# The order of two matrix products per attention head on TensorE, in a four-layer kernel on one core

## The chip, the cores and the metric

The kernel runs on one core of a Trainium2 chip. The metric is the device time of one launch in microseconds. Before the change it is 380.82 us, the median of three runs (380.45 to 381.33). All times below are in us unless they are marked ns.

## The reference

Four residual layers work on x, of 4 batches, 256 rows and 256 columns, each after a layer normalisation: a quantised expert layer, a feed-forward layer with ternary weights, an attention over a small context, and a feed-forward layer with a shared and a routed part. The change is in the attention:

```
q = (text_hidden @ Wq).reshape(B, T_text, N_HEADS, HEAD_DIM).transpose(0, 2, 1, 3)
k = (vision_tokens @ Wk)...      # 8 key/value heads, each used by two of the 16 heads
v = (vision_tokens @ Wv)...
...
attn = softmax(scores / scale)
out = jnp.einsum('bhts,bhsd->bhtd', attn, v)
return out @ Wo                  # summed over the 16 heads
```

A batch has 256 text rows and 256 context rows of 128 columns. The kernel folds Wq with Wk and Wv with Wo before the first attention (a_hi and c_hi below), so a head needs neither keys nor values of its own.

## The kernel before

The four batches run one after the other, and in each the four layers. Every engine has its instructions written out by hand in one fixed order, and semaphores tie the engines together. Products are taken in fp32r on values that are split into a high and a low part, so one product is three passes: high by high, high by low, low by high. The high part is a ScalarE copy out of PSUM, and the low part is a VectorE subtraction that follows it.

The attention of a batch is a loop over its 16 heads. For head h TensorE does the following, in this order (lines 688 to 712):

- turn_probs(h): four 128x128 transposes of the normalised probabilities into the bank pt (L646).
- scores(h+2): six matmuls into a bank s (L626, and L634 for the low part of the queries).
- queries(h+4): six matmuls into half of the bank qa (L418), up to head 11.
- beside(h, 0): pieces of other layers, at a few heads. At head 5 it turns rounded rows of the next batch's expert layer, and at head 12 it forms that layer's second product, both in batches 0 to 2. At head 14 it is the last folded weight in batch 0 (prep_unit, L933) and in batches 1 to 3 a late chunk of the feed-forward layer of the batch before (ffn_up, twelve matmuls of L418 on yt_hi and yt_lo). At head 15 in batches 1 and 2 it is ffn_down of a late chunk.
- project(h-2), from head 2 on: six matmuls into the bank o, four on ut_hi (L681) and then two on ut_lo (L685).
- mix(m), after every odd head up to 13 and after heads 14 and 15: it multiplies the turned probabilities of the heads 2m and 2m+1 with the context into the bank u (L662, L666).
- beside(h, 1): further pieces.

What project reads is made after the mix. ScalarE copies the bank u to ut_hi (mix_hi, L1010; semaphore u_h), and VectorE then subtracts to get ut_lo (mix_lo, L1754; u_l). The pair of heads 2m and 2m+1 is mixed at the end of head 2m+1, and head 2m+2 is the first to project it. So project stands close behind its inputs at the even heads 2 to 14. At an odd head it reads what the even head before it has read already.

What queries writes is copied by ScalarE once a pair is complete, at odd heads (queries_hi, qa_hi), and then VectorE subtracts (queries_lo, qa_lo). At an odd head ScalarE's order is: the turned probabilities (pt_hi), queries_hi, other layers' work, the two exponentials of head h+2 (L1062), and at the next head mix_hi. VectorE's order is: the inverses of the row sums (L1743), mix_lo at an even head, probs_lo (pt_lo), the row minima of the scores (L1735), queries_lo at an odd head, then other layers' work. GpSimd normalises the probabilities (L1355).

Of the kernel before, what the change touches and what calls it, by code (L numbers as in the profile page):

```python
# [78 lines left out]
def build(nc, x_in, gu_in, guT_in, ctx_in, ctxT_in, mask_in, w12T_in, w3T_in, wqT_in, wkT_in,  # L79
          wvT_in, wo_in, routerT_in, gateT_in, upT_in, downT_in, out):  # L80
    with ExitStack() as ctx:
# [19 lines left out]
        def mix_unit(h):  # L101
            return h // 2 if h < H - 2 else h - PAIRS + 1

        def mix_heads(m):
            return (2 * m, 2 * m + 1) if m < PAIRS - 1 else (m + PAIRS - 1,)
# [306 lines left out]
        def _(pe):  # L412
# [173 lines left out]
            def queries(b, h):  # L586

                p = h // 2
                if h % 2 == 0 and p >= 1:
                    pe.wait_ge(S["qa_l"], PAIRS * b + p)  # L590
                if b == 0 and h >= 2 and h % 2 == 0:
                    pe.wait_ge(S["prep_lo"], prep_count(h))
                if b == 0 and h == 1:
                    pe.wait_ge(S["prep_lo"], PREP_BANKS.index("qa", 5) + 1)
                dst = bank["qa"][:, (h % 2) * T:(h % 2 + 1) * T]
                for k in range(ND):
                    last = split_mm(dst, a_hi[:, h, k, :], a_lo[:, h, k, :], xt_hi[:, k, :], xt_lo[:, k, :],
                                    k == 0, k == ND - 1)
                if h % 2 == 1:
                    last.then_inc(S["qa_mm"], 1)  # L600
# [11 lines left out]
            def scores(b, h):  # L612
                if b == 0 and h == 0:
                    pe.wait_ge(S["qa0_h"], 1)
                else:
                    pe.wait_ge(S["qa_h"], PAIRS * b + h // 2 + 1)
                if h >= 2:
                    pe.wait_ge(S["s_min"], NT * (H * b + h - 1))
                elif b == 0:
                    pe.wait_ge(S["prep_lo"], PREP_BANKS.index(("s0", "s1")[h], 4) + 1)  # L620
                dst = bank["s0"] if h % 2 == 0 else bank["s1"]
                ring, col = (h // 2) % 2, (h % 2) * T
                for t in range(NT):
                    cols = slice(col + t * P, col + (t + 1) * P)
                    for half in (cxT_hi, cxT_lo):
                        pe.matmul(dst[:, t * T:(t + 1) * T], qa_hi[:, ring, cols], half[:, :],  # L626
                                  start=(t == 0 and half is cxT_hi), stop=False, skip_group_check=True)
                if b == 0 and h == 0:
                    pe.wait_ge(S["qa0_l"], 1)
                else:  # L630
                    pe.wait_ge(S["qa_l"], PAIRS * b + h // 2 + 1)
                for t in range(NT):
                    cols = slice(col + t * P, col + (t + 1) * P)
                    last = pe.matmul(dst[:, t * T:(t + 1) * T], qa_lo[:, ring, cols], cxT_hi[:, :],  # L634
                                     start=False, stop=True, skip_group_check=True)
                last.then_inc(S["s_mm"], 1)

            def turn_probs(b, h):
                if b == 0 and h == 0:
                    pe.wait_ge(S["prep_lo"], PREP_BANKS.index("pt") + 1)  # L640
                if h >= 1:
                    pe.wait_ge(S["t_l"], H * b + h)
                for t in range(NT):
                    pe.wait_ge(S["s_norm"], NT * (H * b + h) + t + 1)
                    for s in range(2):
                        last = pe.transpose(bank["pt"][:, s * T + t * P:s * T + (t + 1) * P],  # L646
                                            prob[:, h % 2, t, s * P:(s + 1) * P], ident[:, :])
                last.then_inc(S["t_mm"], 1)

            def mix(b, m):  # L650

                heads, cols = mix_heads(m), mix_cols(m)
                pe.wait_ge(S["t_h"], H * b + heads[-1] + 1)
                if m >= 1:
                    pe.wait_ge(S["u_l"], MIXES * b + m)
                elif b > 0:
                    pe.wait_ge(S["shared_x"], b)
                else:
                    pe.wait_ge(S["prep_lo"], PREP_BANKS.index("u", 6) + 1)
                for s in range(2):  # L660
                    for half in (cx_hi, cx_lo):
                        pe.matmul(bank["u"][:, cols], half[:, s, :], pt_hi[:, s, cols], start=(s == 0 and half is cx_hi),  # L662
                                  stop=False, skip_group_check=True)
                pe.wait_ge(S["t_l"], H * b + heads[-1] + 1)
                for s in range(2):
                    last = pe.matmul(bank["u"][:, cols], cx_hi[:, s, :], pt_lo[:, s, cols], start=False, stop=(s == 1),  # L666
                                     skip_group_check=True)
                last.then_inc(S["u_mm"], 1)

            def project(b, h):  # L670
                if b == 0 and h == 0:
                    pe.wait_ge(S["prep_lo"], 2 * PAIRS - 1)
                elif b == 0 and h == H - 2:
                    pe.wait_ge(S["prep_lo"], 2 * PAIRS)
                elif h == 0:
                    pe.wait_ge(S["routed_x"], b)
                pe.wait_ge(S["u_h"], MIXES * b + mix_unit(h) + 1)
                at = (h % 2) * T
                for t in range(NT):
                    for half in (c_hi, c_lo):  # L680
                        pe.matmul(bank["o"][:, t * D:(t + 1) * D], ut_hi[:, at + t * P:at + (t + 1) * P], half[:, h, :],  # L681
                                  start=(h == 0 and t == 0 and half is c_hi), stop=False, skip_group_check=True)
                pe.wait_ge(S["u_l"], MIXES * b + mix_unit(h) + 1)
                for t in range(NT):
                    last = pe.matmul(bank["o"][:, t * D:(t + 1) * D], ut_lo[:, at + t * P:at + (t + 1) * P], c_hi[:, h, :],  # L685
                                     start=False, stop=(h == H - 1), skip_group_check=True)
                last.then_inc(S["o_mm"], 1)

            def attention(b, beside=None):

                for h in range(H):
                    if (b, h) == (NB - 1, 1):
                        scores(b, h + 2)
                        turn_probs(b, h)
                    else:
                        turn_probs(b, h)
                        if h + 2 < H:
                            scores(b, h + 2)
                    if h + 4 < H:
                        queries(b, h + 4)  # L700
                    if beside is not None:
                        beside(h, 0)
                    if h >= 2:
                        project(b, h - 2)
                    if h == H - 1 and b < NB - 1:
                        project(b, H - 2)
                    if h == mix_heads(mix_unit(h))[-1]:
                        mix(b, mix_unit(h))
                    if h == H - 1 and b == NB - 1:
                        project(b, H - 2)  # L710
                    if beside is not None:
                        beside(h, 1)
# [150 lines left out]
            def batch(b, last):  # L863
                def beside(h, part):
# [15 lines left out]
                    if not last and (h, part) == (15, 1):  # L880
                        pe.wait_ge(S["s_min"], NT * H * (b + 1))
                        bit_up(b + 1, 0)
                attention(b, beside)
                if not last:
                    pe.wait_ge(S["t_l"], H * (b + 1))
# [1235 lines left out]
```

## Time and profile before

| what | value |
|---|---|
| median of three runs | 380.82 |
| the profiled execution's own time | 380.73 |
| its span, first to last instruction | 379.0 |
| TensorE busy | 372.3, 98% of the span |
| VectorE, ScalarE, GpSimd busy | 78%, 60%, 44% |
| granted TensorE clock, mean | 0.999 of 2.4 GHz |

The span and what lies around it (1.7) make up the profiled execution's time. TensorE appears as two rows: PE for matmuls and PEld for the loads of their stationary operand. In this kernel a load stands in front of every matmul, and the matmul starts 0.11 to 0.14 behind it in most places. A wait that belongs to a product is seen at the load when the stationary operand is what it waits for, as ut_hi and ut_lo are in project. The start of a load is therefore the place of its matmul on TensorE. The ends of matmuls are modelled.

### The profile page before, as it was taken

Reading aid. Unit: us, or ns where it says so; the run is one execution under the profiler, and the core shown is the slowest. Engines: PE = TensorE matmul, PEld = TensorE weight load, DVE = VectorE, ACT = ScalarE, POOL = GpSimd, SP = SyncE. Lnnn points to the kernel's source line nnn. Section 1 sums busy time; section 2 is a strip of 40 time slices with the busy share of each in tenths; the row PEclk is TensorE's granted clock in tenths of the full one; section 3 lists DMA queues with packets and bytes.
Section 4 is the critical chain, followed back from the end, with each engine's and each line's share of the span. In section 5 each row is a group of like instructions: output and inputs, shape, how many; then the busy total and the mean of one; then the engine's idle time right before and its main releaser. Section 6 shows DMA issues by size and latency. Waiting matters only on the chain.

```text
span 379.0 us, 8383 instructions
## 1 busy us (share of the span) xinstructions
PE 372.3 (98%) x2966; PEld 352.2 (93%) x2966; DVE 296.0 (78%) x969; ACT 229.2 (60%) x611; POOL 165.2 (44%) x263
## 2 busy tenths in 40 slices
PE   8999989999999999999999999999999999999996
PEld 7989879999899999999999999999999999999996
DVE  4789789898867999787767999787768876766655
ACT  1776878867654476767554467667454666764332
POOL 2135676956543345245353435245343243332232
PEclk9999999999999999999999999999999999999999
DMA  6999310000000200000000200000000000000000
GB/s 225 338 353 395 137 33 3 1 2 0 3 2 0 88 0 3 2 1 3 3 28 2 61 1 2 0 3 3 1 29 2 0 3 0 3 0 2 13 19 28
DMA packets 15209, 16.93 MB, mean 45 GB/s; under 512 B 1600, under 2 KB 14144, under 8 KB 15168
## 3 DMA queue, kind: packets, MB, share of 16 engines
q1 hardware_dynamic: 15168, 16.40, 12.8%
q8 instruction: 24, 0.39, 0.4%
q14 instruction: 17, 0.14, 0.1%
HBM read 15.34 MB, written 1.05 MB: 43 GB/s over the span
## 4 chain that ended last, share of the span: by engine, by line
PE 91%; DVE 4%; ACT 2%; POOL 1%; issue 1%; DVEq 0%; POOLq 0%
PE bank_qa L418 12%; PE bank_u L662 8%; PE bank_o L681 8%; PE bank_pt L646 8%; PE bank_s L626 7%; PE bank_s L418 5%; PE bank_u L666 4%; PE bank_o L685 4%; PE bank_s L634 4%; PE bank_s L540 3%; PE bank_pt L418 3%; PE bank_pt L570 3%; PE bank_pt L540 2%; PE bank_u L776 2%; PE bank_x L427 2%; PE bank_u L556 2%
## 5 line engine op out<-in xcount | busy, mean ns | idle before, releaser
L1355 POOL TENSOR_SCALAR prob<-prob,row_inv,valid_b 128x256 f32<-128x256 f32 x128 | 70.6, 561 | 80.9 <-DVE row_inv L1743 80.9
L1062 ACT ACTIVATE prob<-prob,row_min 128x256 f32<-128x256 f32 x128 | 64.2, 503 | 40.3 <-DVE row_min L1735 40.0
L1748 DVE TENSOR_TENSOR pt_lo<-bank_pt,pt_hi 128x512 fp32r<-128x512 f32 x64 | 43.9, 685 | 14.0 <-ACT pt_hi L1010 13.9
L1735 DVE CUSTOM_DVE_ANT_0 prob<-bank_s,masked 128x256 f32<-128x256 f32 x128 | 48.5, 417 | 0.9 <-ACT masked L1044 0.6
L1366 POOL TENSOR_TENSOR act_lo<-act_raw,act_hi 128x256 fp32r<-128x256 f32 x32 | 24.1, 753 | 44.3 <-ACT act_hi L1130 44.2
L1010 ACT ACTIVATE pt_hi<-bank_pt 128x512 fp32r<-128x512 f32 x64 | 37.6, 587 | 4.8 <-PE bank_pt L646 4.6
L646 PE MATMUL bank_pt<-ident,prob 128*128 128x128 f32 x256 | 39.5, 275 | 0.9 <-POOL prob L1355 0.7
L626 PE MATMUL bank_s<-cxT_hi,qa_hi 128*128 128x256 f32 x128 | 37.7, 317 | 0.2 <-DVE c_lo L1975 0.2
L418 PE MATMUL bank_qa<-xt_hi,a_hi 128*128 128x256 f32 x126 | 35.2, 279 | 0.0
L418 PE MATMUL bank_qa<-xt_lo,a_hi 128*128 128x256 f32 x126 | 35.1, 278 | 0.0
L418 PE MATMUL bank_qa<-xt_hi,a_lo 128*128 128x256 f32 x126 | 35.1, 278 | 0.0
L646 PEld LDWEIGHTS bank_pt<-ident,prob 128*128 128x128 f32 x256 | 29.6, 141 | 5.3 <-issue 1.4
L681 PE MATMUL bank_o<-c_hi,ut_hi 128*128 128x256 f32 x128 | 33.5, 285 | 0.0
L626 PE MATMUL bank_s<-cxT_lo,qa_hi 128*128 128x256 f32 x128 | 32.8, 280 | 0.0
L681 PE MATMUL bank_o<-c_lo,ut_hi 128*128 128x256 f32 x128 | 32.6, 278 | 0.0
L1754 DVE TENSOR_TENSOR ut_lo<-bank_u,ut_hi 128x512 fp32r<-128x512 f32 (+1 forms) x36 | 22.5, 625 | 12.7 <-ACT ut_hi L1010 12.7
L1130 ACT CAST act_hi<-act_raw 128x256 fp32r<-128x256 f32 (+1 forms) x37 | 14.7, 399 | 29.3 <-DVE act_raw L1784 29.2
L1010 ACT ACTIVATE ut_hi<-bank_u 128x512 fp32r<-128x512 f32 (+1 forms) x36 | 19.6, 546 | 16.4 <-PE bank_u L666 15.8
L662 PE MATMUL bank_u<-pt_hi,cx_hi 128*128 128x512 f32 (+1 forms) x72 | 26.6, 375 | 0.3 <-ACT pt_hi L1010 0.3
L662 PE MATMUL bank_u<-pt_hi,cx_lo 128*128 128x512 f32 (+1 forms) x72 | 26.3, 370 | 0.0
L685 PE MATMUL bank_o<-c_hi,ut_lo 128*128 128x256 f32 x128 | 25.4, 280 | 0.0
L634 PE MATMUL bank_s<-cxT_hi,qa_lo 128*128 128x256 f32 x128 | 25.3, 279 | 0.0
(349 smaller groups left out, 1182.2 us busy)
## 6 DMA issues: line engine op xcount, KB each, us to landing
wq_raw<-in_wqT SPq DMA_DIRECT2D x4, 512.0 KB, 8.2
wo_raw<-in_wo SPq DMA_DIRECT2D x4, 512.0 KB, 8.0
w_raw<-in_w12T SPq DMA_DIRECT2D x2, 704.0 KB, 7.3
gate_raw<-in_gateT SPq DMA_DIRECT2D x2, 576.0 KB, 7.2
up_raw<-in_upT SPq DMA_DIRECT2D x2, 576.0 KB, 9.1
down_raw<-in_downT SPq DMA_DIRECT2D x2, 576.0 KB, 10.8
guT<-in_guT SPq DMA_DIRECT2D x4, 256.0 KB, 3.5
gu<-in_gu SPq DMA_DIRECT2D x4, 256.0 KB, 2.6
```

The lines of the kernel that those rows point to most:

```text
L418: last = pe.matmul(out_ap, w, r, start=start and n == 0, stop=stop and n == len(passes) - 1, skip_group_check=True)
L626: pe.matmul(dst[:, t * T:(t + 1) * T], qa_hi[:, ring, cols], half[:, :], start=(t == 0 and half is cxT_hi), stop=False, skip_group_check=True)
L634: last = pe.matmul(dst[:, t * T:(t + 1) * T], qa_lo[:, ring, cols], cxT_hi[:, :], start=False, stop=True, skip_group_check=True)
L646: last = pe.transpose(bank["pt"][:, s * T + t * P:s * T + (t + 1) * P], prob[:, h % 2, t, s * P:(s + 1) * P], ident[:, :])
L662: pe.matmul(bank["u"][:, cols], half[:, s, :], pt_hi[:, s, cols], start=(s == 0 and half is cx_hi), stop=False, skip_group_check=True)
L681: pe.matmul(bank["o"][:, t * D:(t + 1) * D], ut_hi[:, at + t * P:at + (t + 1) * P], half[:, h, :], start=(h == 0 and t == 0 and half is c_ ...
L685: last = pe.matmul(bank["o"][:, t * D:(t + 1) * D], ut_lo[:, at + t * P:at + (t + 1) * P], c_hi[:, h, :], start=False, stop=(h == H - 1), ...
L1010: act.activation(dst, src, ACT.Copy, scale=scale).then_inc(done, 1)
L1062: act.activation(row, row, ACT.Exp, scale=-1.0, bias=row_min[:, h % 2, t:t + 1], accum_out=row_sum[:, h % 2, t:t + 1]).then_inc(S["s_exp"], 1)
L1355: pool.tensor_scalar(row, row, row_inv[:, h % 2, t:t + 1], valid_b[:, 0:1], ALU.mult, ALU.mult).then_inc(S["s_norm"], 1)
L1735: dve.tensor_tensor_reduce(out=prob[:, h % 2, t, :], in0=src[:, t * T:(t + 1) * T], in1=masked[:, :], scale=1.0, scalar=3.0e38, op0=ALU.ad ...
L1748: dve.tensor_tensor(pt_lo[:, :, cols], bank["pt"][:, :].rearrange("p (s t) -> p s t", s=2), f32(pt_hi[:, :, cols]), ALU.subtract).then_inc ...
```

## The change

At every head from the third on, project(h-2) is issued before queries(h+4) and beside(h, 0) and not after them. Nothing is added or removed.

```
--- before.py
+++ after.py
@@ -696,12 +696,12 @@
                         turn_probs(b, h)
                         if h + 2 < H:
                             scores(b, h + 2)
+                    if h >= 2:
+                        project(b, h - 2)
                     if h + 4 < H:
                         queries(b, h + 4)
                     if beside is not None:
                         beside(h, 0)
-                    if h >= 2:
-                        project(b, h - 2)
                     if h == H - 1 and b < NB - 1:
                         project(b, H - 2)
                     if h == mix_heads(mix_unit(h))[-1]:
```

On TensorE, at head 6 of the last batch, there stood before (L634 is the end of the scores, L418 the queries, L681 and L685 the projection):

```order
L634 MATMUL bank_s<-cxT_hi,qa_lo 128x256
L418 MATMUL bank_qa<-xt_hi,a_hi 128x256 [waits qa_l]
L418 MATMUL bank_qa<-xt_lo,a_hi 128x256
L418 MATMUL bank_qa<-xt_hi,a_lo 128x256
L418 MATMUL bank_qa<-xt_hi,a_hi 128x256
L418 MATMUL bank_qa<-xt_lo,a_hi 128x256
L418 MATMUL bank_qa<-xt_hi,a_lo 128x256
L681 MATMUL bank_o<-c_hi,ut_hi 128x256 [waits u_h]
L681 MATMUL bank_o<-c_lo,ut_hi 128x256
L681 MATMUL bank_o<-c_hi,ut_hi 128x256
L681 MATMUL bank_o<-c_lo,ut_hi 128x256
L685 MATMUL bank_o<-c_hi,ut_lo 128x256 [waits u_l]
```

The same place of the changed kernel:

```order
L634 MATMUL bank_s<-cxT_hi,qa_lo 128x256
L681 MATMUL bank_o<-c_hi,ut_hi 128x256 [waits u_h]
L681 MATMUL bank_o<-c_lo,ut_hi 128x256
L681 MATMUL bank_o<-c_hi,ut_hi 128x256
L681 MATMUL bank_o<-c_lo,ut_hi 128x256
L685 MATMUL bank_o<-c_hi,ut_lo 128x256 [waits u_l]
L685 MATMUL bank_o<-c_hi,ut_lo 128x256
L418 MATMUL bank_qa<-xt_hi,a_hi 128x256 [waits qa_l]
L418 MATMUL bank_qa<-xt_lo,a_hi 128x256
L418 MATMUL bank_qa<-xt_hi,a_lo 128x256
L418 MATMUL bank_qa<-xt_hi,a_hi 128x256
L418 MATMUL bank_qa<-xt_lo,a_hi 128x256
```

The projection, with its waits on u_h and u_l, now comes directly behind the scores, and the six matmuls of the queries end one projection later.

At head 14 of batch 1 there are no scores and no queries. Before, between the transposes of the probabilities (which stand ahead of this piece) and the projection stood the twelve matmuls of ffn_up, of which these are the last three:

```order
L418 MATMUL bank_qa<-yt_hi,up_hi 128x256
L418 MATMUL bank_qa<-yt_lo,up_hi 128x256
L418 MATMUL bank_qa<-yt_hi,up_lo 128x256
L681 MATMUL bank_o<-c_hi,ut_hi 128x256 [waits u_h]
L681 MATMUL bank_o<-c_lo,ut_hi 128x256
L681 MATMUL bank_o<-c_hi,ut_hi 128x256
L681 MATMUL bank_o<-c_lo,ut_hi 128x256
L685 MATMUL bank_o<-c_hi,ut_lo 128x256 [waits u_l]
L685 MATMUL bank_o<-c_hi,ut_lo 128x256
L662 MATMUL bank_u<-pt_hi,cx_hi 128x256 [waits u_l,t_h]
```

In the changed kernel the projection follows the four transposes (L646):

```order
L646 MATMUL bank_pt<-ident,prob 128x128 [waits s_norm,t_l]
L646 MATMUL bank_pt<-ident,prob 128x128
L646 MATMUL bank_pt<-ident,prob 128x128 [waits s_norm]
L646 MATMUL bank_pt<-ident,prob 128x128
L681 MATMUL bank_o<-c_hi,ut_hi 128x256 [waits u_h]
L681 MATMUL bank_o<-c_lo,ut_hi 128x256
L681 MATMUL bank_o<-c_hi,ut_hi 128x256
L681 MATMUL bank_o<-c_lo,ut_hi 128x256
L685 MATMUL bank_o<-c_hi,ut_lo 128x256 [waits u_l]
L685 MATMUL bank_o<-c_hi,ut_lo 128x256
L418 MATMUL bank_qa<-yt_hi,gate_hi 128x256 [waits ffn_prod]
```

The twelve matmuls of ffn_up stand behind it now. On ScalarE, VectorE, GpSimd and SyncE the order of the instructions is the same in both kernels.

## Rows read from the trace of the kernel before

**Rows 1.** The page's first part: busy time, share, instructions of each engine.
```profile
PE 372.3 (98%) x2966; PEld 352.2 (93%) x2966; DVE 296.0 (78%) x969; ACT 229.2 (60%) x611; POOL 165.2 (44%) x263
```

**Rows 2.** Windows, attention of batch 1: PE, PEld, DVE, ACT, POOL busy, clock, DMA.
```profile
135.00:176.00 41.00, 41.00 (x327) 38.81 (x327) 35.22 (x128) 28.48 (x80) 18.05 (x35) 1.00 0.01 2
```

**Rows 3.** Timeline, last batch, heads 5 and 6: start, duration, engine, line, operation, idle before.
```profile
315.28 0.60 ACT L1010 ACTIVATE qa_hi<-bank_qa 128x512 fp32r<-128x512 f32 x1 [0.45 <-PE bank_qa L418]
...
315.93 0.51 ACT L1062 ACTIVATE prob<-prob,row_min 128x256 f32<-128x256 f32 x1
...
316.44 0.49 ACT L1062 ACTIVATE prob<-prob,row_min 128x256 f32<-128x256 f32 x1
...
317.35 0.60 ACT L1010 ACTIVATE ut_hi<-bank_u 128x512 fp32r<-128x512 f32 x1 [0.32 <-PE bank_u L666]
...
317.98 0.69 DVE L1754 TENSOR_TENSOR ut_lo<-bank_u,ut_hi 128x512 fp32r<-128x512 f32 x1 [0.76 <-ACT ut_hi L1010]
...
318.18 0.19 PEld L418 LDWEIGHTS bank_qa<-xt_hi,a_hi 128*128 128x128 f32 x1
...
318.89 0.19 PEld L681 LDWEIGHTS bank_o<-c_hi,ut_hi 128*128 128x128 f32 x1
...
319.36 0.31 PEld L685 LDWEIGHTS bank_o<-c_hi,ut_lo 128*128 128x128 f32 x2
```

**Rows 4.** Timeline, last batch, head 12.
```profile
337.25 0.69 DVE L1754 TENSOR_TENSOR ut_lo<-bank_u,ut_hi 128x512 fp32r<-128x512 f32 x1 [0.81 <-ACT ut_hi L1010]
...
337.99 0.30 PEld L685 LDWEIGHTS bank_o<-c_hi,ut_lo 128*128 128x128 f32 x2
```

**Rows 5.** Timeline, batch 1, head 14 (ffn_up, ut_lo, projection).
```profile
181.41 0.19 PEld L418 LDWEIGHTS bank_qa<-yt_hi,gate_hi 128*128 128x128 f32 x1
...
182.57 0.67 DVE L1754 TENSOR_TENSOR ut_lo<-bank_u,ut_hi 128x512 fp32r<-128x512 f32 x1
...
182.78 0.19 PEld L681 LDWEIGHTS bank_o<-c_hi,ut_hi 128*128 128x128 f32 x1
...
183.29 0.30 PEld L685 LDWEIGHTS bank_o<-c_hi,ut_lo 128*128 128x128 f32 x2
```

**Rows 6.** Timeline, last batch, head 14.
```profile
343.79 0.69 DVE L1754 TENSOR_TENSOR ut_lo<-bank_u,ut_hi 128x512 fp32r<-128x512 f32 x1 [0.41 <-ACT ut_hi L1010]
...
345.16 0.31 PEld L685 LDWEIGHTS bank_o<-c_hi,ut_lo 128*128 128x128 f32 x2
```

**Rows 7.** Timeline, batch 0, head 14 (the last folded weight, ut_lo, projection).
```profile
99.07 0.73 PEld L933 LDWEIGHTS bank_qa<-wo_raw,wvT 128*128 128x128 f32 x4
...
99.62 0.67 DVE L1754 TENSOR_TENSOR ut_lo<-bank_u,ut_hi 128x512 fp32r<-128x512 f32 x1
...
100.40 0.31 PEld L685 LDWEIGHTS bank_o<-c_hi,ut_lo 128*128 128x128 f32 x2
```

**Rows 8.** Timeline, head 2 of batch 0 and of the last batch.
```profile
59.24 0.68 DVE L1754 TENSOR_TENSOR ut_lo<-bank_u,ut_hi 128x512 fp32r<-128x512 f32 x1
...
60.54 0.31 PEld L685 LDWEIGHTS bank_o<-c_hi,ut_lo 128*128 128x128 f32 x2
...
305.47 0.69 DVE L1754 TENSOR_TENSOR ut_lo<-bank_u,ut_hi 128x512 fp32r<-128x512 f32 x1 [0.32 <-ACT ut_hi L1010]
...
306.32 0.30 PEld L685 LDWEIGHTS bank_o<-c_hi,ut_lo 128*128 128x128 f32 x2
```

**Rows 9.** Timeline, batch 1, head 8.
```profile
161.93 0.67 DVE L1754 TENSOR_TENSOR ut_lo<-bank_u,ut_hi 128x512 fp32r<-128x512 f32 x1
...
163.08 0.31 PEld L685 LDWEIGHTS bank_o<-c_hi,ut_lo 128*128 128x128 f32 x2
```

**Rows 10.** Timeline, batch 1, head 10.
```profile
168.45 0.69 DVE L1754 TENSOR_TENSOR ut_lo<-bank_u,ut_hi 128x512 fp32r<-128x512 f32 x1 [0.24 <-ACT ut_hi L1010]
...
169.77 0.30 PEld L685 LDWEIGHTS bank_o<-c_hi,ut_lo 128*128 128x128 f32 x2
```

**Rows 11.** Timeline of weight loads, last batch, head 1: a load that waits.
```profile
302.49 0.19 PEld L662 LDWEIGHTS bank_u<-pt_hi,cx_hi 128*128 128x128 f32 x1 [0.51 <-ACT pt_hi L1010]
```

More of the change, by code:

```diff
@@ L698, in attention @@
                             scores(b, h + 2)
+                    if h >= 2:
+                        project(b, h - 2)
                     if h + 4 < H:
@@ L702, in attention @@
                         beside(h, 0)
-                    if h >= 2:
-                        project(b, h - 2)
                     if h == H - 1 and b < NB - 1:
```

## The prediction

> **What bounds the kernel now.** I read the page's busy times first. TensorE is busy for 372.3 of a span of 379.0, 98%, far ahead of VectorE's 296.0 [rows 1]. The windows come next: in the attention of batch 1, from 135 to 176, TensorE is busy for 41.00 of 41.00 [rows 2]. There is no idle time in an attention that another order could remove; what a new order can do is open a gap. The third view is the timeline around the projections, where I compare two times: the end of ut_lo on VectorE, and the start of the load that reads it (L685). Their difference is the slack s. At head 6 of the last batch ut_lo ends at 317.98 + 0.69 = 318.67 and the load starts at 319.36, so s = 0.69 [rows 3]. At head 12 of that batch nothing stands between scores and projection already. There ut_lo ends at 337.94 and the load starts at 337.99 [rows 4], and at head 14 of batch 1 the two times are 183.24 and 183.29 [rows 5]. I read 0.05 as the time from the end of ut_lo to the earliest load, because the smallest difference repeats.
>
> **The change, part by part.** No instruction is added or removed, on no queue (no DMA is moved either), so TensorE's own work stays the same. Two things move.
>
> First, the projection loses the cover of what stood ahead of it. With six matmuls of queries that is L = 318.89 - 318.18 = 0.71 [rows 3], and with ffn_up at head 14 it is 182.78 - 181.41 = 1.37 [rows 5]. Behind a waiting projection all of TensorE is queued, and TensorE sets the end.
>
> Second, the queries end one projection later, 0.70 (six loads at the spacing between L681 and L685, 0.47 / 4 [rows 3]). ScalarE waits for them already: before qa_hi it was idle for 0.45, released by the queries [rows 3]. In its queue the two exponentials and then ut_hi stand behind qa_hi. So qa_hi moves from 315.28 to 315.98. One such instruction follows the other after 0.51 (315.93 to 316.44), and three of them bring ut_hi to 315.98 + 3 x 0.51 = 317.51. Before it started at 317.35, after an idle 0.32 that TensorE's mix released [rows 3]. So 0.32 and the wait for the row minima swallow most of it, and a delay D = 0.16 is left.
>
> The loss at one projection is then L + 0.05 + D - s, and not below zero.
>
> - Heads 4, 6, 8, 10 of the last batch: 0.71 + 0.05 + 0.16 - 0.69 = 0.23 each, from head 6 [rows 3], four times 0.92. Head 12 there waits already, so it pays only D, 0.16 [rows 4]. Together 1.08. With D = 0 it would be 0.28, with D = 0.70 (nothing swallowed) 3.8.
> - Head 2 of the four batches. Head 1 has no projection, so its queries don't move and D = 0. Batch 0: s = 60.54 - 59.92 = 0.62, loss 0.14. Last batch: s = 306.32 - 306.16 = 0.16, loss 0.60 [rows 8]. The other two I put between these, so four times the mean of 0.37, 1.48 (bounds 4 x 0.14 and 4 x 0.60).
> - Head 8 of batches 0 to 2: s = 163.08 - 162.60 = 0.48 [rows 9], where VectorE is late with other work. D = 0, and 0.71 + 0.05 - 0.48 = 0.28, three times 0.84. With D = 0.70 it would be 2.9.
> - Heads 4 and 10 of batches 0 to 2, six places: s = 169.77 - 169.14 = 0.63 at head 10 of batch 1 [rows 10]. Here VectorE, too, has work queued between qa_lo and ut_lo, and only 0.24 of idle time ahead of ut_lo to swallow a delay [rows 10]. D lies between 0.16, as above, and 0.70 - 0.24 = 0.46. I take 0.25, nearer to the row that shows the chain whole [rows 3]: 0.38 each, 2.28 (bounds 6 x 0.29 and 6 x 0.59).
> - Heads 6 and 12 of batches 0 to 2: nothing. At head 6 a turning of the next batch stands between mix and projection as extra cover, and at head 12 only that layer's small product is moved behind. Six places, each between 0 and 0.38.
> - Head 14 of the four batches, where there are no scores either and the exponentials of head 15 are the only work ahead of ut_hi, unmoved, so D = 0. In batch 1 the load already starts 0.05 behind ut_lo [rows 5]. Nothing makes ut_lo earlier, so all that stood ahead of the projection and now stands behind it, 1.37, is lost. Batch 2 has the same pieces, 1.37 again. Last batch: s = 345.16 - 344.48 = 0.68 [rows 6], 1.37 + 0.05 - 0.68 = 0.74. Batch 0 moves a folded weight of 0.73 behind the projection [rows 7]. There ut_lo ends at 100.29 and the load started at 100.40, so it can come 0.06 earlier at best, and 0.67 is lost. Sum 4.15.
>
> At odd heads ut_hi and ut_lo have been read one head earlier, so the projection doesn't wait. The scores read qa_lo one head later: at head 6 qa_hi would end at 316.58 and qa_lo 0.7 behind it, while the queries' place after those scores is 318.18 [rows 3]. That cover holds.
>
> The sum is 1.08 + 1.48 + 0.84 + 2.28 + 4.15 = 9.83. The profiled execution took 380.73 (span 379.0), 0.09 under the median of 380.82. So I expect 380.73 + 9.83 = 390.6.
>
> **A rule weighed.** In the last batch a load waits 0.51 for pt_hi, and the view shows it as idle time of the load row, with no later load taken in between [rows 11]. The Trainium skill ("TensorE: Matmul & The Clock Gate", the detail on the array's sub-arrays) says that TensorE's queue is a partial reorder window which can pull weight loads ahead of matmuls in flight, while ScalarE and VectorE are strictly first in, first out. If a later load went ahead during each wait, as the rule allows, a wait would be shorter by one load spacing; that is the second rival. The second half of the rule agrees with the exponentials and ut_hi that stand behind a waiting qa_hi.
>
> **The rivals.**
>
> - Not slower. The wait at a projection could take the place of a later one on TensorE: when the projection waits, the probabilities and the minima of the next head have had that much more time, and TensorE waits less there. The time would stay at 380.7. It decides in favour of this if TensorE had about 0.2 idle or more per pair of heads. The window speaks against it, with 0.00 in 41 [rows 2]; so does slack under 0.76 in all rows shown. Only the 6.7 of idle time in the whole span [rows 1] could be used at all, which is also what a faster kernel could gain at most.
> - Loads go ahead of a waiting projection. Each of some 22 waits (4 + 1 + 4 + 3 + 6 + 4) is shortened by 0.12 (0.47 / 4 [rows 3]), 2.6 in all: 387.9. Rows 11 speak against it.
> - Only heads 2, 8 and 14 pay: 1.48 + 0.84 + 4.15 = 6.5, 387.2. This is so if each wait on TensorE lets VectorE and ScalarE run ahead of it, so that the next pair's ut_lo is early. It needs queues that don't wait for TensorE themselves; in the last batch ut_hi does (0.32 released by the mix [rows 3]), but in batches 0 to 2 VectorE is often busy without a gap [rows 9].
> - The late queries are felt in full. D = 0.70 at the five places of the last batch and 0.59 in place of 0.38 at six others: 5 x 0.54 + 6 x 0.21 = 4.0 more, and head 8 with D = 0.70 2.1 more: 396.7. The idle 0.32 in front of ut_hi [rows 3] speaks against it.
> - That the change doesn't do what it says is excluded by the order of the instructions, which moves on TensorE as described.
>
> **How the numbers follow.** I give the sum 0.58, the loads that go ahead 0.10, the three heads alone 0.17, late queries in full 0.11 and not slower 0.04. The likeliest case is 390.6. Its own range is 388.3 (D = 0 at every place: 4.15 + 1.48 + 0.84 + 6 x 0.13 + 0.28 = 7.5) to 393.9 (heads 4 and 10 at 0.59, + 1.3, heads 6 and 12 at half of their bound, + 1.1, and head 2 at 0.60, + 0.9). The range for 8 in 10 reaches down through 387.2 to 386.5, and up some two thirds of the way to 396.7: 386.5 to 394.5. A measurement of this kernel can tell about 0.2% from no change, 0.76. Faster by more than that has 0.01, within it 0.03 and slower 0.96.
>
> **What would show it.** In the changed kernel the load of ut_lo should start 0.05 behind the end of ut_lo at nearly every even head. Loads of L681 and L685 should head TensorE's list of waits, with some 22 waits, the longest near 1.4 in all at head 14 of batches 1 and 2 (part of it on ut_hi, part on ut_lo). ScalarE's idle time in front of qa_hi should grow by up to 0.70 each, and TensorE's busy share should fall to about 96%, with the granted clock unchanged. I am wrong on the mechanism if TensorE's idle time stays where it is. I am wrong on the sizes if head 14 loses less than 1 in batches 1 and 2, or if the middle heads lose over 0.6 each.

## The result and the profile after

The changed kernel takes 389.48 us (median of 4 runs, 388.96 to 389.65) against 380.92 of the kernel before (median of 4 runs, 380.45 to 381.33). It is slower by a factor of 1.0228, with a 95% interval of 1.0216 to 1.0240. The forecast was 390.6, with a range of 386.5 to 394.5. The profiled execution took 389.39, with a span of 387.7, which is 8.7 longer than before, at a mean granted clock of 1.00.

The page after, its first part and the first line of its chain (share of the span by engine):

```profile
span 387.7 us, 8383 instructions
...
PE 377.9 (97%) x2966; PEld 353.4 (91%) x2966; DVE 298.1 (77%) x969; ACT 225.4 (58%) x611; POOL 165.3 (43%) x263
...
PE 80%; DVE 10%; ACT 5%; issue 3%; POOL 1%; DVEq 0%; POOLq 0%
```

The instruction counts are those of [rows 1], and TensorE is still the longest row. But VectorE and ScalarE have entered the chain, with 10% and 5%; in the kernel before they stood at 4% and 2%, and TensorE at 91%.

The waits of TensorE's weight loads after (us in total, number of waits, longest), the top two rows:

```profile
PEld bank_o L685 <- DVE ut_lo L1754: 4.5, 13, 0.8
PEld bank_o L681 <- ACT ut_hi L1010: 2.0, 4, 0.5
```

The list of before has neither of them. These two are the new waits of the projection. They add up to 6.5; the shorter ones don't show there, as that of 0.16 at head 6 of the last batch (below), and one of 0.3 at head 2 of that batch stands there without a releaser.

Head 14 of batch 1 after, on TensorE's load row (start, duration, then idle time and releaser), to be compared with [rows 5]:

```profile
184.06 0.59 PEld L646 LDWEIGHTS bank_pt<-ident,prob 128*128 128x128 f32 x4
185.14 0.19 PEld L681 LDWEIGHTS bank_o<-c_hi,ut_hi 128*128 128x128 f32 x1 [0.49 <-ACT ut_hi L1010]
...
186.50 0.30 PEld L685 LDWEIGHTS bank_o<-c_hi,ut_lo 128*128 128x128 f32 x2 [0.83 <-DVE ut_lo L1754]
186.73 0.19 PEld L418 LDWEIGHTS bank_qa<-yt_hi,gate_hi 128*128 128x128 f32 x1
...
188.81 0.46 PEld L427 LDWEIGHTS bank_x<-ident,hs 128*128 128x128 f32 x4
```

VectorE at the same place after:

```profile
184.44 0.74 DVE L1491 BATCH_NORM_STATS2 ln_stats<-x 128x6 f32<-128x256 f32 x2
185.28 0.25 DVE L1495 BATCH_NORM_AGGREGATE ln_mv<-ln_stats 128x2 f32<-128x6 f32 x2
185.57 0.17 DVE L1497 TENSOR_SCALAR ln_ve<-ln_mv 128x2 f32<-128x2 f32 x1
185.64 0.22 DVE L1743 RECIPROCAL row_inv<-row_sum 128x1 f32<-128x1 f32 x2
185.78 0.67 DVE L1754 TENSOR_TENSOR ut_lo<-bank_u,ut_hi 128x512 fp32r<-128x512 f32 x1
```

The part with ut_hi waits 0.49 for ScalarE, then the part with ut_lo waits 0.83 for VectorE, which works with hardly a gap (0.10 at most) on another batch's normalisation before it gets to ut_lo. ut_lo ends at 185.78 + 0.67 = 186.45, and the load starts 0.05 behind. The ffn_up loads, which covered this wait before, now stand behind it. No later load was taken during either wait.

To place the loss I compared, in both kernels, the start of the first weight load of each mix (L662); from one mix to the next the shift grows by what the heads in between lost. Rows go by the even head; the odd head behind it is counted in. In us:

```
             batch 0  batch 1  batch 2  last   sum   forecast
head 2         0.02     0.40     0.40   0.39   1.21    1.48
head 4         0.41     0.28     0.31   0.17
head 6         0.03    -0.03    -0.02   0.14
head 8         0.18     0.17     0.23   0.18
head 10        0.24     0.35     0.35   0.14
head 12        0.06    -0.01     0.00   0.04
head 14        0.69     1.38     1.37   0.73   4.17    4.15
head 15        0.13    -0.16    -0.15  -0.03  -0.21    0
4, 6, 8, 10 of the last batch                  0.63    0.92
4 and 10 of batches 0 to 2                     1.94    2.28
8 of batches 0 to 2                            0.58    0.84
6 and 12 of batches 0 to 2                     0.03    0
12 of the last batch                           0.04    0.16
between batches                                0.26    0
total                                          8.65    9.83
```

From the last mix to the end the shift stays what it is (8.67 at the end).

### The profile page after: what moved, and what is told of

It reads as the page before. It is cut to its first block, busy times and chain, and to the rows that moved or that the text cites. A ratio compares the mean times of both kernels' runs of the same rounds, so it can differ in the third digit from the quotient of the medians.

```text
span 387.7 us, 8383 instructions
## 1 busy us (share of the span) xinstructions
PE 377.9 (97%) x2966; PEld 353.4 (91%) x2966; DVE 298.1 (77%) x969; ACT 225.4 (58%) x611; POOL 165.3 (43%) x263
## 3 DMA queue, kind: packets, MB, share of 16 engines
HBM read 15.34 MB, written 1.05 MB: 42 GB/s over the span
## 4 chain that ended last, share of the span: by engine, by line
PE 80%; DVE 10%; ACT 5%; issue 3%; POOL 1%; DVEq 0%; POOLq 0%
PE bank_qa L418 11%; PE bank_o L681 6%; PE bank_pt L646 6%; PE bank_s L626 6%; PE bank_u L662 5%; PE bank_s L418 5%; PE bank_o L685 5%; PE bank_s L540 3%; PE bank_pt L418 3%; PE bank_pt L570 3%; PE bank_s L634 3%; PE bank_u L666 3%; ACT prob L1062 2%; PE bank_pt L540 2%; PE bank_u L776 2%
## 5 line engine op out<-in xcount | busy, mean ns | idle before, releaser
L646 PE MATMUL bank_pt<-ident,prob 128*128 128x128 f32 x256 | 39.0, 273 | 0.8 <-POOL prob L1355 0.7
L418 PE MATMUL bank_qa<-xt_hi,a_hi 128*128 128x256 f32 x126 | 35.1, 278 | 0.0
L418 PE MATMUL bank_qa<-xt_hi,a_lo 128*128 128x256 f32 x126 | 35.0, 278 | 0.0
L418 PE MATMUL bank_qa<-xt_lo,a_hi 128*128 128x256 f32 x126 | 35.0, 278 | 0.0
L681 PE MATMUL bank_o<-c_hi,ut_hi 128*128 128x256 f32 x128 | 33.5, 286 | 1.2 <-ACT ut_hi L1010 1.2
L646 PEld LDWEIGHTS bank_pt<-ident,prob 128*128 128x128 f32 x256 | 29.8, 141 | 4.8 <-issue 1.3
L1010 ACT ACTIVATE qa_hi<-bank_qa 128x512 fp32r<-128x512 f32 (+1 forms) x32 | 18.8, 588 | 26.1 <-PE bank_qa L418 26.1
L681 PE MATMUL bank_o<-c_lo,ut_hi 128*128 128x256 f32 x128 | 32.5, 278 | 0.0
L685 PE MATMUL bank_o<-c_hi,ut_lo 128*128 128x256 f32 x128 | 27.5, 297 | 1.8 <-DVE ut_lo L1754 1.3
L1716 DVE TENSOR_TENSOR qa_lo<-bank_qa,qa_hi 128x512 fp32r<-128x512 f32 x31 | 21.4, 689 | 8.0 <-ACT qa_hi L1010 7.9
L662 PE MATMUL bank_u<-pt_hi,cx_hi 128*128 128x512 f32 (+1 forms) x72 | 27.1, 381 | 0.3 <-ACT pt_hi L1010 0.3
```

Source lines behind the costliest of these rows:

```text
L418: last = pe.matmul(out_ap, w, r, start=start and n == 0, stop=stop and n == len(passes) - 1, skip_group_check=True)
L1010: act.activation(dst, src, ACT.Copy, scale=scale).then_inc(done, 1)
```

## The experiments

Theory W is that of the prediction: each loss is a wait of the moved projection for ut_hi or ut_lo. Rival Q: the late queries hold ScalarE, and that costs. Rival O: every exchange costs the same. Theory V, on head 14: half of its loss in batches 1 and 2 comes from what stands ahead of ut_lo in VectorE's queue. The sizes that theory W expects are mostly taken from the table above; what the runs can tell is whether each loss stays at its place. The edits are shown against the kernel before unless the text says otherwise.

**Head 14 alone, and all but head 14.** The first is

```
+                    if h >= 2 and h == 14:
+                        project(b, h - 2)
                     ...
-                    if h >= 2:
+                    if h >= 2 and not (h == 14):
                         project(b, h - 2)
```

and the second has `h != 14` in both places.

> The projection is moved at head 14 of each batch alone (in front of the last folded weight in batch 0 and of ffn_up in batches 1 to 3). Theory W (each loss is a wait of the moved projection for ut_hi and ut_lo): the four losses of head 14 add up to 4.2 (0.7, 1.4, 1.4, 0.7), a little comes back at head 15 (0.15 in batches 1 and 2), so 384.9 (384.5 to 385.3). Theory Q (the queries that end later at odd heads hold back ScalarE): no queries move, 380.9. Theory O (every exchange of two products costs the same, 8.6 over 56 moved projections, 0.15 each): four of them, 381.5.

> The projection is moved at every head from 2 on except head 14. Theory W: the rest of the loss, 8.6 - 4.2 = 4.4, so 385.3 (384.9 to 385.7). Theory Q: all of it, 389.5. Theory O: 52 of 56 parts, 388.9.

They took 385.59 and 385.48, both 1.0127 times the kernel before (1.0112 to 1.0142, and 1.0114 to 1.0140). With head 14 alone that head loses 0.70, 1.38, 1.37 and 0.76 in the four batches, as in the full change. With all but head 14 it loses nothing, and the shift is 4.59 at the last mix. The load waits of the kernel with head 14 alone:

```profile
PEld bank_o L685 <- DVE ut_lo L1756: 2.1, 4, 0.8
PEld bank_o L681 <- ACT ut_hi L1012: 2.0, 4, 0.5
```

Four waits each, one for each batch, add up to 4.1, and the four losses to 4.2. Four exchanges of 56 make half of the slowdown, so O falls. The two kernels add up by place, nearly: heads 2 to 12 of the second lose 4.14 and head 14 of the first 4.21, together 8.35, and the same heads of the full change 4.45 + 4.17 = 8.62. Most of the difference is at head 2 (0.96 for 1.21). By time they add up to more, 9.9 against 8.56, and the first is 0.3 above its expected range. The surplus stood where the code is the same: 0.30 and 0.35 before the first mix, and 0.55 and 0.28 in the last feed-forward part (see the end).

**Odd heads alone, even heads alone.** At even heads the projection is the first reader of a pair's ut_lo; at odd heads it waits for nothing new, but the queries that complete qa_hi come late. The same edit with `h % 2 == 1`, then with `h % 2 == 0`.

> The projection is moved at odd heads alone (28 of 56 places). There ut_hi and ut_lo have been read a head earlier, but the queries of the pair end one projection (0.70) later. Theory W: nothing waits at the projection, and the late ut_hi (0.16 by my sum) is covered by a slack of 0.6, so 380.9 within 0.4. Theory Q: the whole loss, 389.5. Theory O: half, 385.2.

> The projection is moved at even heads alone. The queries that complete a pair (at odd heads) stay where they are, so D = 0. Theory W: head 14 4.2, head 2 1.2, head 8 0.6, heads 4 and 10 of batches 0 to 2 about 1.3 in place of 1.9, heads 4 to 10 of the last batch 0.3 in place of 0.6; with 0.2 given back 7.4, so 388.3 (387.6 to 388.9). Theory Q: 380.9. Theory O: 385.2.

Odd heads alone: 381.28, ratio 1.0018 (1.0009 to 1.0026), and no head moves by more than 0.1. Of the 0.36 shift at the last mix, 0.35 is there before the first mix. Even heads alone: 387.32, ratio 1.0177 (1.0164 to 1.0190), which is 0.3 under the expected range; the reason stands below. ScalarE with odd heads alone, last batch, heads 5 and 6 (the code stands two lines lower here):

```profile
316.25 0.60 ACT L1012 ACTIVATE qa_hi<-bank_qa 128x512 fp32r<-128x512 f32 x1 [1.05 <-PE bank_qa L418]
...
317.72 0.58 ACT L1012 ACTIVATE ut_hi<-bank_u 128x512 fp32r<-128x512 f32 x1
```

VectorE and the load of ut_lo there:

```profile
318.34 0.69 DVE L1756 TENSOR_TENSOR ut_lo<-bank_u,ut_hi 128x512 fp32r<-128x512 f32 x1 [0.32 <-ACT ut_hi L1012]
```

```profile
319.64 0.31 PEld L685 LDWEIGHTS bank_o<-c_hi,ut_lo 128*128 128x128 f32 x2
```

The late queries are real: ScalarE's idle time ahead of qa_hi is 1.05 instead of 0.45 [rows 3]. But ut_lo ends at 319.03 and its load starts at 319.64, so 0.61 of the 0.69 of slack is left. The delay D that comes through is 0.08, and alone it costs nothing: the 0.18% between the medians shows at no head. Q as a cost of its own falls.

The pair also tests the formula, loss = L + 0.05 + D - s and not below zero. Even heads alone have no late queries. Heads 4 and 10 of batches 0 to 2 lose 0.44 there in six places (theory W expected 1.3), the full change 1.94, and odd heads alone nothing. So the two halves of the change don't add up: odd heads alone stay inside the slack, even heads alone are only 0.07 a place beyond it, and then each delay counts in full. The difference between full change and even heads alone is 1.50 / 6 = 0.25 a place. Head 4 of batch 1 shows what lies behind it. The end of ut_lo and the load that reads it, in the kernel before:

```profile
147.63 0.67 DVE L1754 TENSOR_TENSOR ut_lo<-bank_u,ut_hi 128x512 fp32r<-128x512 f32 x1
...
148.62 0.31 PEld L685 LDWEIGHTS bank_o<-c_hi,ut_lo 128*128 128x128 f32 x2
```

with even heads alone:

```profile
148.63 0.68 DVE L1756 TENSOR_TENSOR ut_lo<-bank_u,ut_hi 128x512 fp32r<-128x512 f32 x1
...
149.36 0.30 PEld L685 LDWEIGHTS bank_o<-c_hi,ut_lo 128*128 128x128 f32 x2
```

and with the full change:

```profile
148.28 0.69 DVE L1716 TENSOR_TENSOR qa_lo<-bank_qa,qa_hi 128x512 fp32r<-128x512 f32 x1 [0.21 <-ACT qa_hi L1010]
...
150.01 0.67 DVE L1754 TENSOR_TENSOR ut_lo<-bank_u,ut_hi 128x512 fp32r<-128x512 f32 x1
...
150.74 0.30 PEld L685 LDWEIGHTS bank_o<-c_hi,ut_lo 128*128 128x128 f32 x2 [0.32 <-DVE ut_lo L1754]
```

The slack before was 0.32 here, not 0.63, because VectorE came late to ut_lo (its row has no idle time ahead). The mix that feeds it started at 144.91, 146.28 and 147.34 in the three kernels, so ut_lo ended 3.39, 3.03 and 3.34 behind its mix. With even heads alone the earlier waits of TensorE let VectorE catch up, by 0.36. With the full change VectorE waits 0.21 for the late qa_hi, and what it had caught up is lost again.

**Only the part with ut_hi goes ahead.** The project function is split; its four matmuls with ut_hi go ahead of the queries, the two with ut_lo stay behind them.

```
-            def project(b, h):
+            def project(b, h, parts=(0, 1)):
...
+                    if h >= 2:
+                        project(b, h - 2, (0,))
                     ...
-                        project(b, h - 2)
+                        project(b, h - 2, (1,))
```

> Only the four matmuls of the projection that read ut_hi are moved ahead, at every head from 2 on. The two that read ut_lo stay behind the queries and the pieces of other layers. Theory W (the price is the wait for ut_lo, and only where it is later than its new place): at head 14 the moved part waits 0.5 for ut_hi in each batch, at head 2 0.1 and 0.35 in batch 1 and the last, else nothing, and ut_lo always finds its old cover: 2.5 in all, 383.1 (382.6 to 383.8). If every exchange costs the same whatever it waits for, as under theory O with two thirds of the projection moved: 386.3. If the queries' delay counted (four matmuls later in place of six): 386.3 as well.

It took 382.86, ratio 1.0054 (1.0037 to 1.0071). Batch 1, head 14, loads:

```profile
182.22 0.19 PEld L682 LDWEIGHTS bank_o<-c_hi,ut_hi 128*128 128x128 f32 x1 [0.49 <-ACT ut_hi L1014]
...
182.69 0.19 PEld L418 LDWEIGHTS bank_qa<-yt_hi,gate_hi 128*128 128x128 f32 x1
...
184.05 0.30 PEld L687 LDWEIGHTS bank_o<-c_hi,ut_lo 128*128 128x128 f32 x2
```

With the ffn_up back between the parts the 0.83 is gone, and the 0.49 for ut_hi stays. Head 14 loses 0.51, 0.47, 0.46 and 0.51. Only head 2 of the other heads loses still (0.19, 0.31 and 0.24 in batches 1, 2 and the last, where the load starts 0.11 behind the end of ut_hi); its batch 0 gains 0.11. The shift is 2.03 of 8.65. So three quarters of the slowdown are waits for ut_lo, and the rest, mostly at head 14, for ut_hi.

**ut_lo ahead of the statistics.** To test V, the changed kernel with one more edit on VectorE (against the changed kernel): the next batch's statistics move from head 13 to behind ut_lo of head 14, in batches 0 to 2.

```
+                    if h == 14 and b < NB - 1:
+                        ln_stats_of(b + 1, "lnb")
...
-                    elif h == 13:
-                        ln_stats_of(nxt, "lnb")
```

> The changed kernel, and on VectorE in batches 0 to 2 the statistics of the next layer's normalisation (1.2 long) go behind mix_lo of head 14 and not ahead of it. Theory V (half of the 1.4 lost at head 14 of batches 1 and 2 is VectorE's queue, not the mix itself): the wait for ut_lo there falls from 0.83 to about 0.17. The normalised rows and, behind them on GpSimd, the probabilities of head 15 come later by 1.2, so TensorE waits 0.3 to 0.5 at their transposes: net 0.2 to 0.4 per batch, 388.9 (388.4 to 389.4). If the queue did not matter, the wait stays at 0.83 and the time is 389.5 or more.

It took 390.98, ratio 1.0268 (1.0254 to 1.0282): slower than the changed kernel, where V expected it faster. Batch 1, heads 14 and 15, loads:

```profile
186.85 0.30 PEld L685 LDWEIGHTS bank_o<-c_hi,ut_lo 128*128 128x128 f32 x2 [0.19 <-DVE ut_lo L1754]
...
189.56 0.20 PEld L427 LDWEIGHTS bank_x<-ident,hs 128*128 128x128 f32 x2 [0.32 <-DVE hs L1502]
190.12 0.20 PEld L427 LDWEIGHTS bank_x<-ident,hs 128*128 128x128 f32 x2 [0.36 <-DVE hs L1502]
```

and the list of load waits of the whole kernel:

```profile
PEld bank_o L685 <- DVE ut_lo L1754: 3.2, 13, 0.3
PEld bank_x L427 <- DVE hs L1502: 2.7, 8, 0.6
PEld bank_o L681 <- ACT ut_hi L1010: 2.0, 4, 0.5
```

The half of V on the cause holds: without the statistics ahead of ut_lo the wait at head 14 falls from 0.83 to 0.19, and the loss there from 1.38 to 0.76 in batch 1. The half on the time falls. The same statistics feed the normalised rows hs, which the next batch's turning (L427) reads at head 15. They come late now, and the wait returns as 0.32 + 0.36, so that in batches 1 and 2 gain and loss cancel (0.62 saved at head 14 of each, 0.68 and 0.61 lost at head 15). In batch 0 the edit saves nothing (ut_lo's wait is 0.19 there, 0.20 before the edit), and head 15 loses 1.46 more than in the changed kernel:

```profile
103.13 0.30 PEld L666 LDWEIGHTS bank_u<-pt_lo,cx_hi 128*128 128x128 f32 x2 [0.49 <-DVE pt_lo L1748]
...
104.01 0.20 PEld L427 LDWEIGHTS bank_x<-ident,hs 128*128 128x128 f32 x2 [0.58 <-DVE hs L1502]
104.57 0.20 PEld L427 LDWEIGHTS bank_x<-ident,hs 128*128 128x128 f32 x2 [0.36 <-DVE hs L1502]
```

**The projection in the middle of the queries.** At heads 2 to 11 it stands between the two halves of the queries, with three matmuls ahead of it and three behind; at heads 12 to 15 it stays where it was before.

```
-            def queries(b, h):
+            def queries(b, h, between=None):
...
+                    if k == 1 and between is not None:
+                        between()
...
-                        queries(b, h + 4)
+                        queries(b, h + 4, (lambda: project(b, h - 2)) if h >= 2 else None)
...
-                    if h >= 2:
+                    if h >= 2 and h + 4 >= H:
                         project(b, h - 2)
```

> Dose: at heads 2 to 11 the projection stands between the first three and the last three matmuls of the queries, so half of the cover is left (0.35 in place of 0.71); at heads 12, 13 and 15 it stands where the change put it or before, without queries, and head 14 is as before. Theory W with its slack: 0.35 + 0.05 + D is under the slack of most places; head 2 of the last batch loses 0.25, head 10 of batch 0 0.2, head 12 nothing, so 381.2 (380.8 to 381.8). If the loss went with the distance moved, half of the 4.9 of the run without head 14: 383.0. If the exchange itself cost (theory O), 385.0.

It took 380.99, ratio 1.0009 (1.0000 to 1.0018): the same as before, within what can be told. No head loses over 0.1, but for one of 0.21 at head 15 of batch 0. With half of the cover, L = 0.36, the formula gives 0.36 + 0.05 + 0.08 - 0.69, below zero at heads 4 to 10 of the last batch. So half of the queries is cover enough there. At head 2 of the last batch, where the slack was only 0.16, a wait is left but not a loss. Loads there:

```profile
306.14 0.19 PEld L683 LDWEIGHTS bank_o<-c_lo,ut_hi 128*128 128x128 f32 x1
306.46 0.30 PEld L687 LDWEIGHTS bank_o<-c_hi,ut_lo 128*128 128x128 f32 x2
...
307.05 0.46 PEld L648 LDWEIGHTS bank_pt<-ident,prob 128*128 128x128 f32 x4
```

The step from 306.14 to 306.46 is 0.32 instead of 0.12, a wait of 0.2 for ut_lo. The transposes then start without a wait. In the kernel before they had one of nearly that size:

```profile
306.81 0.42 PEld L646 LDWEIGHTS bank_pt<-ident,prob 128*128 128x128 f32 x4 [0.18 <-DVE pt_lo L1748]
```

## Why the prediction was right

The mechanism and the sign were right. The forecast lies 1.1 above the measured 389.5, inside the range, and it is that near in part by luck: at heads 4 and 10 of batches 0 to 2 two wrong terms nearly cancel. By its steps:

- **Slack, then 0.05 behind ut_lo.** In the changed kernel the load of ut_lo starts 0.05 to 0.06 behind its end at nearly all even heads. Exceptions are head 6 of batches 1 and 2, which keep 0.7 of slack, and head 6 of batch 0 and head 12 of batches 0 to 2, at 0.13 to 0.14. These are the heads that the prediction put at nothing, and they lost 0.03 in all. That leaves 22 loads right behind ut_lo, the number of waits that the prediction gave; the list shows the 13 longer ones, and at head 14 the 4 for ut_hi ahead of them.
- **Head 14: 4.17 for 4.15.** Each of the four batches came within 0.02, because there every term was a difference between two rows. The head after it gave back 0.16 and 0.15 in batches 1 and 2, which the sum had not counted. Before, the turning at head 15 waited for the normalised rows; after, that load group starts at 188.81 without a wait. The row of before:

```profile
184.72 0.20 PEld L427 LDWEIGHTS bank_x<-ident,hs 128*128 128x128 f32 x2 [0.23 <-DVE hs L1502]
```

- **The delay D of the late queries: over-sized in the last batch, 0.06 to 0.08 for 0.16.** Heads 4 to 10 there lost 0.63 for 0.92, with even heads alone 0.39; the difference of 0.24 over four is 0.06. ScalarE after, last batch, heads 5 and 6, to be compared with [rows 3]:

```profile
323.41 0.60 ACT L1010 ACTIVATE qa_hi<-bank_qa 128x512 fp32r<-128x512 f32 x1 [1.23 <-PE bank_qa L418]
323.91 0.50 ACT L1062 ACTIVATE prob<-prob,row_min 128x256 f32<-128x256 f32 x1
...
324.40 0.50 ACT L1062 ACTIVATE prob<-prob,row_min 128x256 f32<-128x256 f32 x1
...
324.89 0.58 ACT L1010 ACTIVATE ut_hi<-bank_u 128x512 fp32r<-128x512 f32 x1
```

  From qa_hi to ut_hi it is 1.48, where the prediction put 3 x 0.51 = 1.53. With odd heads alone qa_hi comes 0.68 later than before (316.25 - 0.29 of shift - 315.28), where it put 0.70. Two steps of a few hundredths halve a difference that is itself small. The loads after show that the wait is there all the same:

```profile
325.62 0.19 PEld L681 LDWEIGHTS bank_o<-c_hi,ut_hi 128*128 128x128 f32 x1
...
326.25 0.30 PEld L685 LDWEIGHTS bank_o<-c_hi,ut_lo 128*128 128x128 f32 x2
326.48 0.19 PEld L418 LDWEIGHTS bank_qa<-xt_hi,a_hi 128*128 128x128 f32 x1
```

  From L681 to L685 it is 0.63, where it was 0.47 [rows 3].
- **Heads 4 and 10 of batches 0 to 2: 1.94 for 2.28, near by luck.** The prediction took one slack, 0.63, from head 10 of batch 1, and one D, 0.25, a choice between two bounds. The slack before was 0.57, 0.31 and 0.38 at head 4 of the three batches, and 0.25, 0.63 and 0.63 at head 10. Against the kernel before, ut_lo came later behind its mix by 0.25, -0.06, 0.02, -0.15, 0.24 and 0.25. So at three places slack and D were about right, and at the other three both were too large; there ut_lo had been late already, behind VectorE's other work, and the late queries did not make it later. With the six slacks and D = 0.25 the formula gives 3.29, with both as measured 2.34. The rest was given back on TensorE (see head 2), 0.14 of it at head 10 of batch 0, where a delay of 0.36 at the load is 0.22 at the next transposes. Where D was 0.25, it came the way of the prediction's upper bound and not of its lower one: ut_hi was only 0.08 to 0.09 later, but qa_lo waited on VectorE for the late qa_hi, and from there VectorE worked on to ut_lo almost without a gap.
- **Head 8 of batches 0 to 2: 0.58 for 0.84.** Even heads alone lose 0.26, 0.25 and 0.24 there, near the forecast 0.28. The full change loses nearly that at the wait itself: 0.25 at the transposes of head 9 in batch 1. Behind them the same twelve matmuls of head 9, in the other order, take 1.36 (167.61 to 168.97) against 1.41 before (164.70 to 166.11), with no wait in either. It is the same in batch 0; in batch 2 they take 1.36 in both kernels. With odd heads alone, which have the new order at head 9 too, they take 1.41 in batches 0 and 1. So about half of what is missing in these two batches is TensorE's pace (see the end), and what sets it the runs don't show.
- **Head 2: 1.21 for 1.48.** In the last batch it cost 0.39, not 0.60. The step that failed is that a wait at the projection is all loss: the 0.18 that the transposes waited for pt_lo in the kernel before is gone after, because the queries now stand between. This is the first rival, "not slower", true at single places, worth some 0.2 here. The prediction had dismissed it by a window of batch 1, which says nothing of the last batch.
- **The other rivals.** "Loads go ahead" falls by the rows: no later load was taken during the waits of 0.49 and 0.83. "Only heads 2, 8 and 14" falls by the 1.94 at heads 4 and 10, though its mechanism, VectorE catching up while TensorE waits, is what even heads alone show there. "Late queries in full" falls by the odd heads alone.
- **The signs named.** ScalarE's idle time ahead of qa_hi rose from 9.5 to 26.1 over 26 waits. Only 20 of them stand behind a moved projection; these grew by 0.63 each with odd heads alone, near the 0.70, and by 0.85 with the full change, where TensorE's waits at the even heads come on top. TensorE's busy share fell less than said, to 97%: its busy time rose from 372.3 to 377.9 with the same instructions. The window of batch 1's attention after (columns as in [rows 2]) is still nearly full:

```profile
137.00:181.00 44.00, 43.81 (x344) 40.66 (x343) 37.38 (x134) 28.58 (x82) 18.06 (x35) 1.00 0.01 2
```

  The ends of matmuls are modelled, and the matmul ahead of a waiting one covers the first part of the wait: at head 14 of batch 1 the load row shows 0.83, and TensorE's own row only this:

```profile
186.50 0.50 PE L685 MATMUL bank_o<-c_hi,ut_lo 128*128 128x256 f32 x2 [0.63 <-DVE ut_lo L1754]
```

  A wait of 0.2 or less doesn't show there at all. So the busy share was the wrong sign to name, and 41.00 of 41.00 before did not exclude short waits either; the load row and the shifts of the mixes are the ones to read.

## What to carry to other kernels

Before an instruction is moved ahead of others on the bound engine, read the slack of each of its operands at every place where it runs: the end of the producer against the start of the reader. What stood between is cover, and the loss is cover plus handover plus the producer's own delay less the slack, not below zero, and less what a later wait gives back. A slack read at one place doesn't hold at the next. Two halves of an edit can each fit into the slack and together not. An edit that makes one operand early makes the next one in its producer's queue late, so find out who reads that before counting the gain.

## What the runs showed of the hardware

The same twelve ffn matmuls ran at two paces at a granted clock of 1.00, without a wait in between. Start of two neighbouring groups in the last feed-forward part, before:

```profile
357.82 0.19 PEld L418 LDWEIGHTS bank_s<-yt_hi,gate_hi 128*128 128x128 f32 x1
...
359.18 0.19 PEld L418 LDWEIGHTS bank_pt<-yt_hi,gate_hi 128*128 128x128 f32 x1
```

and in the kernel with head 14 alone, where this part is the same code:

```profile
362.45 0.19 PEld L418 LDWEIGHTS bank_s<-yt_hi,gate_hi 128*128 128x128 f32 x1
...
363.87 0.19 PEld L418 LDWEIGHTS bank_pt<-yt_hi,gate_hi 128*128 128x128 f32 x1
```

1.36 against 1.42 for twelve. Over that part it made 0.55 of that kernel's time. Both paces occur in each kernel, in different stretches; what sets them stays open, and differences of half a us between kernels can't be put down to an edit here without the shifts of the mixes beside them.
